# Residual layer pair on one Trainium2 core: loads in pairs, turns moved, fc1 begun ahead of the last turn, and a copy moved from VectorE to ScalarE

## What is computed

```python
x = x + (einsum('bsd,bdh->bsh', x, W[cat_ids]) + b[cat_ids])          # layer 0, gives y
h = gelu(einsum('bnd,hd->bnh', x, fc1_w) + fc1_b)                     # 512 -> 2048
shared = einsum('bnh,sh->bns', h, fc2_w) + fc2_b                      # 2048 -> 384
expert = einsum('bnh,bph->bnp', h, experts_w[ids]) + experts_b[ids]   # 2048 -> 128
x = x + concatenate([shared, expert], axis=-1)
```

## Time and profile before

| | us |
|---|---|
| median of 3 runs | 1657.6 |
| lowest, highest | 1655.45, 1658.23 |
| the profiled execution | 1657.96 |
| its span, first to last instruction | 1656.2 |

### The profile page before, as it was taken

One profiled execution on the slowest core, in us unless ns is written; L12 is line 12 of the kernel. 1 busy time (PEld: TensorE's weight loads), 2 busy tenths in 40 slices (PEclk: granted clock), 3 DMA queues, 4 the chain that ended last, 5 costly groups with the idle time before them and its releaser, 6 DMA issues.

```text
span 1656.2 us, 27997 instructions
## 1 busy us (share of the span) xinstructions
PE 1637.2 (99%) x7064; PEld 1320.6 (80%) x7064; DVE 1314.8 (79%) x2004; ACT 554.1 (33%) x926; POOL 214.4 (13%) x195
## 2 busy tenths in 40 slices
PE   7999999999999999999999999999999999999999
PEld 4788887888888888888888888888888887888887
DVE  5787978788787887877878788787878878788865
ACT  4343333333333333333333333333333333333321
POOL 0110200202020120200202011020200202002100
PEclk8899999999999999999999999999999999999999
DMA  7665555546465454664546555454654546555410
GB/s 218 175 187 136 164 151 155 144 139 167 130 175 145 143 157 115 174 161 142 153 115 183 146 161 142 141 159 133 168 157 135 152 114 180 162 144 148 134 52 26
DMA packets 303178, 243.44 MB, mean 147 GB/s; under 512 B 34152, under 2 KB 234984, under 8 KB 303084
## 3 DMA queue, kind: packets, MB, share of 16 engines
q1 hardware_dynamic: 255852, 203.75, 45.1%
q10 hardware_dynamic: 47232, 38.82, 7.7%
HBM read 209.93 MB, written 32.51 MB: 146 GB/s over the span
## 4 chain that ended last, share of the span: by engine, by line
PE 97%; issue 1%; SPq 1%; DMA 1%; DVE 1%; ACT 0%; DVEq 0%
PE ps_out L812 42%; PE ps_e L797 21%; PE ps_h L797 21%; PE ps_y L784 10%; PE ps_t L745 1%; PE ps_h L784 0%; SPq L316 0%; DMA x_blocks<-in_x 0%; DMA e_blocks<-in_L_cond_W 0%; DMA exps<-in_itok_B 0%; SPq L348 0%; PE ps_e L745 0%; PE ps_h L782 0%; DVE w_split L602 0%; DVE y L637 0%
## 5 line engine op out<-in xcount | busy, mean ns | idle before, releaser
L812 PE MATMUL ps_out<-w2e,h 128*128 128x512 f32 x3072 | 756.6, 395 | 0.0
L812 PEld LDWEIGHTS ps_out<-w2e,h 128*128 128x128 f32 x3072 | 575.5, 188 | 137.8
L797 PE MATMUL ps_e<-y_t,w 128*128 128x512 f32 x1536 | 378.2, 396 | 0.5 <-DVE y_t L602 0.5
L797 PE MATMUL ps_h<-y_t,w 128*128 128x512 f32 x1536 | 376.4, 394 | 0.0
L797 PEld LDWEIGHTS ps_e<-y_t,w 128*128 128x128 f32 x1536 | 289.1, 189 | 68.9 <-issue 3.8
L797 PEld LDWEIGHTS ps_h<-y_t,w 128*128 128x128 f32 x1536 | 289.6, 189 | 65.3
L646 DVE STREAM_TRANSPOSE e_whole<-e_blocks 128x512 f32<-128x512 f32 x256 | 279.1, 1090 | 0.0
L528 ACT CAST w2e<-e_whole 128x512 fp32r<-128x512 f32 x256 | 158.7, 620 | 355.3 <-DVE e_whole L646 355.3
L671 DVE CAST h<-g_raw 128x512 fp32r<-128x512 f32 x256 | 125.6, 491 | 182.8 <-ACT g_raw L542 182.7
L461 POOL TENSOR_TENSOR x_raw<-x_raw,b_all 128x512 f32<-128x512 f32 x60 | 87.3, 1455 | 1286.3 <-DMA x_raw<-in_x 1238.5
L497 ACT CAST w_split<-w_raw 128x512 fp32r<-128x512 f32 x244 | 145.2, 619 | 213.3 <-DMA w_raw<-in_L_cond_W 122.5
(11 more groups left out here) (68 smaller groups left out, 459.3 us busy)
## 6 DMA issues: line engine op xcount, KB each, us to landing
e_blocks<-in_L_cond_experts_w SPq DMA_DIRECT2D x1024, 64.0 KB, 2.5
w_raw<-in_L_cond_W SPq DMA_DIRECT2D x248, 256.0 KB, 4.0
out<-resid SPq DMA_DIRECT2D x64, 256.0 KB, 2.6
b_all<-in_L_cond_b SPq DMA_DIRECT2D x60, 256.0 KB, 4.2
x_raw<-in_x SPq DMA_DIRECT2D x60, 256.0 KB, 4.7
x_blocks<-in_x SPq DMA_DIRECT2D x240, 64.0 KB, 3.2
y_rows<-y ACTq DMA_DIRECT2D x60, 256.0 KB, 3.5
x_blocks<-y_rows ACTq DMA_DIRECT2D x240, 64.0 KB, 2.7
```

The costliest lines, as they stand in the source:

```text
L797: last = nc.tensor.matmul(h_bank(c)[:, :], w1[:, w, k, c * P:(c + 1) * P], y_t[:, a, k, :, :].rearrange("p b s -> p (b s)"), start=(k == 0 ...
L812: last = nc.tensor.matmul(ps_out[b][:, :], h[:, c % 2, a, b * S:(b + 1) * S], fc2_columns(c, c % 2, w, b), start=(c == 0 and n == 0), stop ...
```

## The change

- SP asks for both index tables at once and waits for the expert indices only behind all of layer 0's weights. Slices 0 to 3 are loaded singly, the others in pairs by one transfer of 512 KB (`FIRST_W`, `load_first_w`). A bias row is loaded behind its batch's slices, the next input behind it. The first input and fc1's bias are asked for by ScalarE; the preparation tiles 1 to 3 are asked for one by one in the steps j = 0 to 2.
- On TensorE the next input is turned behind slice k = 0 (before: k = 1), the bias row stands before slice k = 1 (k = 3), y's turn behind the third slice of the next batch (the first), the preparation tiles one each at j = 4, 7, 10, 13 (2, 5, 8, 11).
- fc1's first two steps are computed for the first three batches (384 columns) as soon as their y is ready: half of step 0 ahead of the last batch's turn, the rest behind it (`fc1_ahead`). The last batch's 128 columns follow in `fc1`. The turn of tile 5 comes behind all this.
- In step 0 ScalarE takes tile 5 ahead of the gelu, and VectorE lowers it ahead of `h_high`.
- `copy_last` is ScalarE's, behind `e_high` and ahead of the gelu, in all 256 steps.
- The second preparation tile of a step is lowered ahead of the transpose of the next step's experts.
- The first experts of the second quad are loaded in step 0, the expert bias of the next group in step 11 (before: 15).

```diff
+    FIRST_W = ((0,), (1,), (2,), (3,), (4, 5), (6, 7), (8, 9), (10, 11), (12, 13), (14, 15))
...
-            return [t for t in range(1, PREP_FIRST) if j == PSLOTS * t - 1]
+            return [t for t in range(1, PREP_FIRST) if j == PSLOTS * t + 1]
...
+            def load_first_w(n, cat):
+
+                j, m = FIRST_W[n][0], len(FIRST_W[n])
+                after(sp, w_lo, j + m - W0SLOTS)
...
+                sp.dma_start(dst.rearrange("p k n -> p (k n)"), src).then_inc(w0_in[n], 16)
...
+            sp.dma_start(exps[:, :], exp_ids.rearrange("(o n) -> o n", o=1)).then_inc(exps_in, 16)
             sp.wait_ge(cats_in, 16)
+            for n, slices in enumerate(FIRST_W):
+                b = slices[0] // KD
+                if slices[0] % KD == 0:
+                    cat = category(0, b)
+                load_first_w(n, cat)
+                if slices[-1] % KD == KD - 1:
+                    sp.dma_start(b0_rows[:, b, :], l0_b[bass.ds(cat, 1), :]).then_inc(b0_rows_in[b], 16)
+                    if b + 1 < GB:
+                        load_first_x(b + 1)
+            sp.wait_ge(exps_in, 16)
...
+            def copy_last(g, c):
+
+                after(act, fc2_done, (g * NC + c - 1) * GB)
+                if first(g) and c % 4 == 0:
+                    act.wait_ge(prep_lo, prep_count("fc2", NS - 1, c // 4))
+                nc.scalar.copy(ring[:, c % 2, :, :, 1, :],
+                               w2[:, :, c, SHARED - P:].unsqueeze(2).to_broadcast([P, 2, GB // 2, P]))\
+                    .then_inc(last_ready, 1)
...
-            for t in range(PSLOTS):
-                load_prep(act, t)
+            act.dma_start(resid[:, 0, :], x[0, :, :]).then_inc(first_x_in[0], 16)
+            load_prep(act, 0)
+            act.dma_start(b1[:, :].rearrange("p (u c) -> p u c", c=QUAD), fc1_b.rearrange("(u p c) -> p u c", p=P, c=QUAD))\
+               .then_inc(b1_in, 16)
...
                     e_high(g, c)
+                    copy_last(g, c)
...
+                    if c == 0:
+                        prep_high(prep_in_step(g, c, 0))
                     gelu(g, c)
...
-                    copy_last(g, c)
                     e_low(g, c)
...
+                    if c == 0:
+                        prep_low(prep_in_step(g, c, 0))
                     h_high(g, c)
-                    prep_low(prep_in_step(g, c, 0))
+                    if c > 0:
+                        prep_low(prep_in_step(g, c, 0))
                     h_low(g, c)
+                    prep_low(prep_in_step(g, c, 1))
                     turn_next_e(g, c, more)
-                    prep_low(prep_in_step(g, c, 1))
...
-                if first(G) and k == KD - 1:
+                if first(G) and k == 1:
...
+            def fc1_part(c, at, end, tiles):
+
+                for k in tiles:
+                    for n, (a, w) in enumerate(((0, 0), (1, 0), (0, 1))):
+                        last = nc.tensor.matmul(h_bank(c)[:, at * S:end * S], w1[:, w, k, c * P:(c + 1) * P],
+                                                y_t[:, a, k, at:end, :].rearrange("p b s -> p (b s)"),
+                                                start=(k == 0 and n == 0), stop=(k == KD - 1 and n == 2))
+                return last
...
+                fc1_part(c, GB - 1 if first(g) and c < 2 else 0, GB, range(KD)).then_inc(fc1_done, 1)
...
-                if j % KD == 1 and j // KD + 1 < GB:
+                if j % KD == 0 and j // KD + 1 < GB:
                     turn_x(j // KD + 1)
-                if j % KD == 0 and j > 0:
+                if j % KD == KD - 2 and j > KD:
                     turn_y(j // KD - 1)
+            fc1_ahead(0, range(KD // 2))
             turn_y(GB - 1)
+            fc1_ahead(0, range(KD // 2, KD))
+            fc1_ahead(1, range(KD))
```

More of the change, by code:

```diff
@@ L115, in build @@
         prep_in = [sem(f"prep_in{i}") for i in range(PSLOTS)]
-        w0_in = [sem(f"w0_in{i}") for i in range(W0SLOTS)]
+        w0_in = [sem(f"w0_in{i}") for i in range(len(FIRST_W))]
         w_in = [sem(f"w_in{i}") for i in range(WSLOTS)]
@@ L440, in body @@
                         load_expert_bias(0, first_experts)
-                    if more and c == NC - 1:
-                        load_expert_bias(g + 1, next_idx)
                 if not more:
@@ L492, in w_high @@
                 if first(G):
-                    act.wait_ge(w0_in[j % W0SLOTS], 16 * (j // W0SLOTS + 1))
+                    act.wait_ge(w0_in[[j in slices for slices in FIRST_W].index(True)], 16)
                 else:
@@ L657, in e_low @@
                       experts_of(c % 2, 0)).then_inc(e_lo, 1)
-            def copy_last(g, c):
-                after(dve, fc2_done, (g * NC + c - 1) * GB)
-                if first(g) and c % 4 == 0:
-                    dve.wait_ge(prep_lo, prep_count("fc2", NS - 1, c // 4))
-                nc.vector.tensor_copy(ring[:, c % 2, :, :, 1, :],
-                                      w2[:, :, c, SHARED - P:].unsqueeze(2).to_broadcast([P, 2, GB // 2, P]))\
-                    .then_inc(last_ready, 1)
             def h_high(g, c):
@@ L794, in fc1 @@
                 after(pe, gelu_done, g * NC + c - 1)
-                for k in range(KD):
-                    for n, (a, w) in enumerate(((0, 0), (1, 0), (0, 1))):
-                        last = nc.tensor.matmul(h_bank(c)[:, :], w1[:, w, k, c * P:(c + 1) * P],
-                                                y_t[:, a, k, :, :].rearrange("p b s -> p (b s)"),
-                                                start=(k == 0 and n == 0), stop=(k == KD - 1 and n == 2))
-                last.then_inc(fc1_done, 1)
+                fc1_part(c, GB - 1 if first(g) and c < 2 else 0, GB, range(KD)).then_inc(fc1_done, 1)
             def fc2(g, c):
```

73 lines of the change are left out of this document (32 added, 41 removed).

## The result

The changed kernel took 1660.26 us (median of 9 runs, 1657.34 to 1664.01), the kernel before 1655.61 us (9 runs, 1654.23 to 1658.58) beside it: 1.0029 times as long, 95% interval 1.0020 to 1.0038. So it is slower by 0.3%, where 1649.3 us was forecast and slower had a chance of 0.03. The profiled execution took 1661.0 us, with a span of 1659.2 us; the one before had 1656.2.

What follows compares the result with a forecast made beforehand. TensorE, busy 1637.2 of 1656.2 us, was taken as the bound, with only the opening before the first fc2 having much to give. -9.3 + 1.0 - 0.1 = -8.4 us gave about 1649.3 us, range 1645.0 to 1654.3.

Steps and rivals of the forecast that it cites:

- part 4: First group, second tile's low part before experts' turn: TensorE waits about 1.0 us more in step 2; later loads cost 0.
- Part 1: Layer 0 of the first group: last slice ends at 32.8 us, 5.6 us earlier, from fewer waits and less low clock.
- Part 2: From the last slice to the first fc2: 12.2 us instead of 15.7, so fc2 starts at 44.8 us, 9.3 us earlier.
- the lower level: Opening, TensorE clock at 1.2 of 2.4 GHz: extra time in layer 0 falls from 3.8 to 2.0 us.
- second rival: Opening: the clock falls again or transfers land slowly, costing 2.5 us, so 1651.8 us; chance 0.15.
- first rival: Opening's fc1: products of 128 columns cost 0.118 us, not 0.231; 2.1 us less, 1647.2 us; chance 0.15.
- The wait for tile 7: Opening, before fc2: if small products are cheap, tile 7 waits for tile 6 behind the gelu, giving back 0.6 us.
- Part 3: Copy of w2's last columns moved from VectorE to ScalarE: worth 0 in steady groups, covered by ScalarE's slack.
- the wait at 86 us: First group, TensorE's 1.39 us wait behind a VectorE burst beside GpSimd: counted -0.1 us, bounds -1.4 and +1.
- The slower case: Steady groups: ScalarE sets the pace through the copy before every gelu, 12.6 us more, 1661.9 us; chance 0.03.

Runs made afterwards that it cites:

- the three orders put right: Changed kernel with GpSimd's first addition held until the first fc2 step, turn's new order in step 0 alone, y's additions in free steps: 1649.48 us, 0.9950 of before.

## Why the prediction was wrong

**The step that failed** is the last sentence of part 4: the loads of later experts and of the expert bias in other steps are due several steps later: 0. The loads were never late, and that was all I looked at. I did not ask what stands behind them on SP's queue. The load of expert 0 stood there with a wait, and the next group's input stood behind it, so it was the brake of GpSimd's addition. Taken back alone it gives 6.9 us; in the traces the ends of 14 groups lose 9.6 us with the load moved and 1.3 with it back, against a forecast of 0. That the addition is what costs there, the run with the addition held shows: 2.4 us with all transfers as early.

**Parts 1 and 2** together came out at 9.46 us instead of 9.3. That is in part luck, for two errors offset each other. **Part 1** was right on the transfers (no idle time before slice 4) and short on the clock: the last slice ended at 34.2 us, not 32.8, though the first had started 0.5 us early. The term that was mis-sized is the lower level, put at 2.0 us with bounds of 1.3 and 3.8. It measured 4.0: 0.7 for the first three products, 0.4 for a turn, 0.95 for the bias row and 2.0 for nine products up to 17.6 us. The prediction had named the mechanism, a row of products broken up and a later rise. So most of the 2.5 us of its second rival came, but by the later rise, not by another fall. **Part 2** had its error the other way. Twelve products of 128 columns cost 1.29 us, 0.11 each, not 0.231, so 3.0 us less for both rows of twelve: the first rival was right in its price, below even the turn's 0.118. The wait for tile 7 that it named is there as well (0.44 us). The Trainium skill (TensorE: Matmul & The Clock Gate, Back-to-back issue gap) gives about 81 ns for such a product; these 24 took 108, so the trace does not agree, and the measurement decides.

But 9.46 us is not what the median gains. The profiled execution of before, against which I made the sum, had one of the slower openings: the median of the kernel before was 1655.6 us here and 1655.8 to 1656.6 in the later comparisons, 1.4 to 2.4 us below that execution. And the clock has a large part in it. In the profiled execution of before, the lower level cost 7.8 us up to the first fc2: 3.8 as the prediction counted, and 4.0 in the 24 fc1 products and a turn behind the last slice, which part 2 priced at the full level without saying that this was a gain of the clock. In the changed kernel it cost 4.0 us. So some 3.8 of the 9.46 us are the clock's; the forecast had 1.8 + 4.0 in it. Against an old opening whose clock does not fall (47.2 us) the new one is only 2.5 us ahead.

**Part 3**, the copy, was right to 1.2 us: 0.09 us at each group's end. I had looked for its cover at step 1, where 2.8 us lie between gelu and fc2, not at the end of the group, where fewer than 1 us do.

**Part 4** forecast 1.0 us more for step 2 and 0.1 us less for the wait at 86 us, with bounds up to 1.5 and 1 us more. The waits were 1.49 us (none before) and 1.96 us (1.39 before), both within the bounds, but the first group lost 4.25 us in all: 2.1 in its first two steps, 0.6 each in steps 4 and 8, and 1.0 at its end, where the addition and a block of y for which VectorE waited 2.13 us come together. A wait of 0.47 us at 48 us, those of step 8 and the end were in no term. The order of turn and low part is worth 1.6 us, in steps 4 and 8. What makes the wait in step 2 stays open. GpSimd's additions, which had lain ahead of the first fc2 in the kernel before (49 to 53 us) and now, with fc2 9.5 us earlier, lie in its second step, may have a part in it; the run that moved them does not show it.

**The rivals.** The slower case had the right sign and, with 1661.9 us, nearly the time, but another mechanism: ScalarE is at 41%, and no gelu of a middle step was late. None of the rivals took up that a transfer moved forward triggers another engine. With the three orders put right the kernel takes 1649.5 us: the gain that the forecast counted is there, and was given back at the ends of the groups and in the first one. That this is so near to the forecast's 1649.3 is luck in part. Its profiled execution gains 10.5 us up to the first fc2, not 9.3, and 0.8 in the first group, where 0.9 was to be lost; it loses 2.6 at the ends and gains 1.3 in the other steps of the groups, both forecast as 0.

## What to carry to other kernels

A wait on a queue is also a brake for all that stands behind it. Before it is removed or moved, list what it held back, down to the engine that starts when those transfers land, and look where that work falls now. A slack has to be read at its smallest: at the ends of loops, where the step that covers it elsewhere is missing. And a sum against one profiled execution wants a second one: where the granted clock falls in the part to be changed, the two may be 7 us apart. A clock of 1.00 in a stage is to be checked against the prices of its products, for the record of the clock may begin later.

## What was not expected of the hardware

- Beside an addition on GpSimd that takes 1.3 us alone, VectorE's operation of 0.69 us with two inputs in SBUF took 1.65 us, and the addition itself 1.48. The second group, with such a meeting and a block of y that came 1.3 us late, took 1.6 us longer.
- An SP queue with a loop stands 2.4 to 4.2 us at each branch back and some 0.7 us at each index read; in three of the programs 1.4 to 1.8 us are lost again within the reads. Where a queue has under 2 us to spare, that shows in the time (1677 us in one run).
- The old opening, with the same instructions on TensorE, ended 7 us earlier in an execution in which the granted clock did not fall. What decides that from one execution to the next stays open.
- In the new opening the lower level lasted to 17.65 us, 5.5 us longer than in the old one (12.18), and cost 4.0 us.
